# Gate with columns on partitions, bias and gate applied out of PSUM, and rank products ahead of the output products in a recurrence

## What is computed

```python
r = xr @ W_r
log_w = -softplus(-(tanh(xw @ w_lora_a) @ w_lora_b + w_lora_bias)) - 0.5
k = xk @ W_k
v = xv @ W_v
a = sigmoid(xa @ a_lora_a @ a_lora_b + a_lora_bias)
g = sigmoid(r @ g_lora_a) @ g_lora_b + g_lora_bias
...
def step(S, xs):                      # S: (batch, head, 16, 16), 1024 steps
    r_t, w_t, k_t, v_t, a_t, b_t = xs
    sa = einsum('bhij,bhj->bhi', S, a_t)
    S = S * exp(w_t)[:, :, None, :] + sa[..., None] * b_t[:, :, None, :] \
        + v_t[..., None] * k_t[:, :, None, :]
    o_t = einsum('bhij,bhj->bhi', S, r_t)
...
o_flat = ((o - mu) * rsqrt(var + EPS)).reshape(Bn, Tn, C) * gn_weight + gn_bias
bonus = ((rh * kh * r_k).sum(-1, keepdims=True) * vh).reshape(Bn, Tn, C)
return (o_flat + bonus) * g @ W_o
```

## Time and profile before

| | |
|---|---|
| median of 3 runs | 4384.21 us |
| profiled execution | 4389.97 us, its span 4388.2 us |
| PE busy | 3922.4 us (89%) |
| DVE busy | 3172.3 us (72%) |
| ACT busy | 2217.2 us (51%) |
| POOL busy | 2087.8 us (48%) |
| mean granted TensorE clock | 0.938 |
| recurrence: first and last `prod` start | 2234.7 and 3841.4 us |

### The profile page before, as it was taken

How to read it: one execution, slowest core, us unless ns; L and a number is a source line. 1 busy time by engine, 2 the same in 40 slices (tenths; PEclk the granted TensorE clock), 3 DMA queues, 4 the chain that set the end, 5 groups by cost and what they waited for, 6 DMA issues and landing times. The chain is left out here.

```text
span 4388.2 us, 71340 instructions
## 1 busy us (share of the span) xinstructions
PE 3922.4 (89%) x23332; PEld 2675.2 (61%) x23332; DVE 3172.3 (72%) x8603; ACT 2217.2 (51%) x7429; POOL 2087.8 (48%) x1686
## 2 busy tenths in 40 slices
PE   5999999999996599698959999999999999947698
PEld 2344444444344466466648888888888888846465
DVE  5778777777763311599869999999999999957310
ACT  1666666666665311466504655555555556524211
POOL 2212211211212522223358888888888888725322
PEclk7999999999996699799979999999999999977799
DMA  4323322332344332344452232232232322157242
GB/s 111 79 75 78 96 73 66 102 79 59 88 112 135 125 125 85 116 181 174 170 108 36 35 42 36 35 43 35 38 41 35 41 37 35 22 174 250 68 132 79
DMA packets 478766, 378.35 MB, mean 86 GB/s; under 512 B 298348, under 2 KB 440713, under 8 KB 472260
## 3 DMA queue, kind: packets, MB, share of 16 engines
q1 hardware_dynamic: 466116, 348.64, 32.5%
q0 software_dynamic: 12288, 25.28, 1.8%
HBM read 221.87 MB, written 159.58 MB: 87 GB/s over the span
## 5 line engine op out<-in xcount | busy, mean ns | idle before, releaser
L750 DVE TENSOR_REDUCE at_neg_max<-at_slot 128x1 f32<-128x512 f32 (+3 forms) x1216 | 745.8, 655 | 247.9 <-PE at_slot L542 245.1
L672 ACT ACTIVATE at_prob<-at_slot 128x512 f32<-128x512 f32 (+1 forms) x1216 | 631.3, 577 | 356.1 <-PE at_slot L562 355.3
L2157 PE MATMUL sc_added<-sc_outer,sc_ident 128*128 128x128 f32 x4096 | 585.6, 286 | 63.4 <-POOL sc_outer L1908 42.8
L2157 PEld LDWEIGHTS sc_added<-sc_outer,sc_ident 128*128 128x128 f32 x4096 | 496.4, 191 | 193.9 <-DVE sc_state L2058 115.4
L1921 POOL TENSOR_TENSOR sc_terms<-sc_seen,sc_pack 128x1024 f32<-128x1024 f32 (+2 forms) x288 | 603.1, 2137 | 13.7 <-PE sc_ps_o L2179 13.7
L2179 PE MATMUL sc_ps_o<-sc_terms,sc_ident 128*128 128x256 f32 x2048 | 607.0, 381 | 2.1 <-POOL sc_terms L1921 2.1
L390 POOL TENSOR_SCALAR_AFFINE_SELECT at_prob<-at_prob 128x512 f32<-128x512 f32 x256 | 163.5, 639 | 889.3 <-ACT at_prob L672 889.2
L2081 ACT ACTIVATE sc_seen<-sc_state 128x512 f32<-128x512 f32 x256 | 152.9, 597 | 744.0 <-DVE sc_decayed L2022 733.5
L542 PE MATMUL at_slot<-at_k_stack,at_q_stack 96*128 96x512 bf16 (+3 forms) x1536 | 459.5, 335 | 22.5 <-DMA at_k_stack<-parts 20.1
L1908 POOL TENSOR_TENSOR sc_outer<-sc_pack 128x2048 f32<-128x2048 f32 x128 | 467.3, 3672 | 5.0
L562 PE MATMUL at_slot<-at_q_stack,at_k_stack 99*128 99x512 bf16 (+3 forms) x1536 | 452.9, 331 | 12.2 <-ACT at_prob L672 11.8
(11 more groups left out here) (311 smaller groups left out, 7144.5 us busy)
## 6 DMA issues: line engine op xcount, KB each, us to landing
packed<-pr_pack SPq DMA_DIRECT2D x16, 3072.0 KB
sc_pack<-packed SPq DMA_DIRECT2D x512, 96.0 KB, 3.6
parts<-at_parts SPq DMA_DIRECT2D x96, 256.0 KB
f_up_w<-in_ffn_wi SPq DMA_DIRECT2D x16, 1024.0 KB
f_down_w<-in_ffn_wo SPq DMA_DIRECT2D x16, 1024.0 KB
at_q_stack<-parts SPq DMA_DIRECT2D x32, 384.0 KB
at_k_stack<-parts SPq DMA_DIRECT2D x32, 384.0 KB
slots<-at_no_row SPq DMA_DIRECT2D x2, 4128.0 KB
```

Of the source, the lines that this page charges most:

```text
L672: act.activation(prob[:, first:first + n, q1 - tiles * P:q1], ps[:, 0:n * tiles * P].rearrange("p (n k) -> p n k", n=n), ACT.Exp)\
L750: dve.tensor_reduce(neg_max[:, chunk, qt, h:h + n], ps[:, 0:n * tiles * P].rearrange("p (n k) -> p n k", n=n), AX.X, ALU.max, negate=True) ...
L2157: pe.matmul(added[h][:, 0:HALF], ident[:], outer[m % 2][:, 2 * n + s, h * HALF:(h + 1) * HALF], start=(s == 0), stop=False)
```

## The change

In `prepare` the gate is made with columns on partitions: TensorE multiplies the weights `inner_b["g"]` as the stationary operand with all 1024 tokens, one half of the columns per job; ScalarE empties it with the bias as a per-partition column, and it is stored as (batch, half, column, token).

In `finish_and_route` GpSimd has no bias job. VectorE makes o * weight + bonus, TensorE turns it, and VectorE takes each turned piece of 128x512 out of PSUM with (+ bias, * gate) in one operation into `y_turned`; ScalarE copies no longer. The job list is in another order: `y_turn` and `r_turn` before `weigh_o` of the next batch, `place` before `y_out`, `choose` before `affine`.

In `recurrence` (1) on TensorE `rank` comes before both `terms` products of a pair; (2) GpSimd adds the outer products of the two steps for pairs 1 and 3 of each half span, after each half's outer products, and TensorE has one matmul per half state instead of two for these four of eight pairs; (3) ScalarE writes `seen` with i and j exchanged, and GpSimd's product reads and writes in that order, with r repeated along the innermost dimension, where before the output was written with a step of 16.

```diff
 FINISH_SLOTS = 6
-FINISH_USER = {"y_turn": "act", "y_out": "dve", "r_turn": "act"}
+FINISH_USER = {"y_turn": "dve", "y_out": "dve", "r_turn": "act"}
 def finish_plan():
...
         return [(stage, (b, c, half)) for half in range(2) for c in range(KC)]
-    plan = of("bias", 0) + of("weigh_o", 0)
+    plan = of("weigh_o", 0)
     for b in range(BATCH + 2):
-        plan += of("bias", b + 1) + of("weigh_o", b + 1) + of("weigh", b - 2) + parts("y_turn", b) + parts("r_turn", b - 1)
-        plan += of("count", b - 2) + parts("y_out", b) + of("gate", b - 1) + of("place", b - 2) + of("stats", b)
-        plan += of("affine", b) + of("choose", b - 1)
+        plan += of("weigh", b - 2) + parts("y_turn", b) + of("count", b - 2) + parts("r_turn", b - 1) + of("weigh_o", b + 1)
+        plan += of("place", b - 2) + parts("y_out", b) + of("gate", b - 1) + of("stats", b)
+        plan += of("choose", b - 1) + of("affine", b)
     return plan
                 k = b % 2
-                for dst, src in ((o, feed.o_in), (bonus, feed.bonus_in), (og, feed.gate_in)):
+                for dst, src in ((o, feed.o_in), (bonus, feed.bonus_in)):
                     sp.dma_start(dst[k][:], rows(src, b)).then_inc(in_ready[k], 16)
+                sp.dma_start(og[k][:], feed.gate_in[b].rearrange("k p t -> p k t")).then_inc(in_ready[k], 16)
             def load_x(b):
                 sp.dma_start(x[b % XBUFS][:], rows(x_in, b)).then_inc(x_loaded[b % XBUFS], 16)
-            bias_wide = wide_b[:].unsqueeze(1).broadcast_to([P, TILES, C])
-
             for stage, what, s, use in plan.jobs:
-                if stage == "bias":
-                    b = what
-                    if b == 0:
-                        pool.wait_ge(norm_in, 1 + 32)
-                    pool.wait_ge(in_ready[b % 2], 1 + 48 * (b // 2 + 1))
-                    pool.tensor_tensor(bonus[b % 2][:], bonus[b % 2][:], bias_wide, ALU.add).then_inc(with_bias, 1)
-                elif stage == "place":
+                if stage == "place":
                     b = what
...
                     if (c, half) == (0, 0):
-                        pe.wait_ge(gated, 1 + b + 1)
+                        pe.wait_ge(weighed_o, 1 + b + 1)
                     for n in range(HALF_TILES):
...
                     act.activation(exps[b % 2][:], work[:], ACT.Exp).then_inc(exp_ready, 1)
-                elif stage in ("y_turn", "r_turn"):
+                elif stage == "r_turn":
                     b, c, half = what
...
                     if b and (c, half) == (0, 0):
-                        if stage == "y_turn":
-                            slots.wait_read(act, *[("y_out", (b - 1, q)) for q in range(4)])
-                        else:
-                            act.wait_ge(gate_ready, 1 + b)
-                    dst = y_turned if stage == "y_turn" else turned
-                    act.activation(dst[:, c, half * BANK:(half + 1) * BANK], slot[s][:], ACT.Copy)\
+                        act.wait_ge(gate_ready, 1 + b)
+                    act.activation(turned[:, c, half * BANK:(half + 1) * BANK], slot[s][:], ACT.Copy)\
                        .then_inc(emptied[s], 1)
...
                 own.link(dve.tensor_tensor(o[k][:], o[k][:], weight_wide, ALU.mult))
-                dve.wait_ge(with_bias, 1 + b + 1)
-                own.link(dve.tensor_tensor(o[k][:], o[k][:], bonus[k][:], ALU.add))
-                dve.tensor_tensor(o[k][:], o[k][:], og[k][:], ALU.mult).then_inc(gated, 1)
+                dve.tensor_tensor(o[k][:], o[k][:], bonus[k][:], ALU.add).then_inc(weighed_o, 1)
+
+            def gate_y(b, c, half, s, use):
+                slots.wait_filled(dve, s, use)
+                if b and (c, half) == (0, 0):
+                    slots.wait_read(dve, *[("y_out", (b - 1, q)) for q in range(4)])
+                columns = slice(half * BANK, (half + 1) * BANK)
+                dve.scalar_tensor_tensor(out=y_turned[:, c, columns], in0=slot[s][:], scalar=norm_b[:, c:c + 1],
+                                         in1=og[b % 2][:, c, columns], op0=ALU.add, op1=ALU.mult)\
+                   .then_inc(emptied[s], 1)
             def add_x(b, quarter, s, use):
...
         OPS = 10
-        AHEAD = 10
+        AHEAD = 12
+        SUMMED = (1, 3)
         BEHIND = 5
...
                         pack[m % 4][:, t, FK * D:(FK + 1) * D].unsqueeze(2).broadcast_to(shape), ALU.mult))
+                    own.done()
+                    by_steps = outer[m % 2][:, t, :].rearrange("p (a q s) f -> p a q s f", q=2, s=2)
+                    of_pairs = by_steps[:, :, SUMMED[0]]
+                    own.up(pool.tensor_tensor(of_pairs[:, :, 0, :], of_pairs[:, :, 0, :], of_pairs[:, :, 1, :], ALU.add))
                 assert own.n + 2 == AHEAD
...
                     return pool.tensor_tensor(
-                        terms[m % 2][:].rearrange("p (n s) (j i) -> p n s i j", s=2, j=D)[:, pair:pair + n, step],
-                        seen[:, slot:slot + n, :].rearrange("p n (i j) -> p n i j", j=D),
-                        vectors(m, step, FR)[:, pair:pair + n, :].unsqueeze(2).broadcast_to(shape), ALU.mult)
+                        terms[m % 2][:].rearrange("p (n s) (j i) -> p n s j i", s=2, j=D)[:, pair:pair + n, step],
+                        seen[:, slot:slot + n, :].rearrange("p n (j i) -> p n j i", j=D),
+                        vectors(m, step, FR)[:, pair:pair + n, :].unsqueeze(3).broadcast_to(shape), ALU.mult)
                 first = m % 2 * PAIRS
...
                     if pair == 0:
-                        dve.wait_ge(pre, 1 + g * AHEAD + AHEAD - 2)
+                        dve.wait_ge(pre, 1 + g * AHEAD + AHEAD - 4)
                     for h in range(2):
...
                 slot, to = (m * PAIRS + pair) % RING, m % 2 * PAIRS + pair
-                act.activation(seen[:, to:to + 2, :], state[:, slot:slot + 2, :], ACT.Copy).then_inc(copied, 1)
+                act.activation(seen[:, to:to + 2, :].rearrange("p n (j i) -> p n i j", j=D),
+                               state[:, slot:slot + 2, :].rearrange("p n (i j) -> p n i j", j=D), ACT.Copy)\
+                   .then_inc(copied, 1)
             def copy_o(g):
...
                 if n in (0, PAIRS // 2):
-                    pe.wait_ge(pre, 1 + g * AHEAD + AHEAD - 1 + n // (PAIRS // 2))
+                    pe.wait_ge(pre, 1 + g * AHEAD + AHEAD - 2 + n // (PAIRS // 2) * 2)
                 for h in range(2):
                     pe.wait_ge(chain, CHAIN + 1 + (g * PAIRS + n - 1) * OPS + OPS - 1 + h)
-                    for s in range(2):
+                    for s in range(1 if n % (PAIRS // 2) in SUMMED else 2):
                         pe.matmul(added[h][:, 0:HALF], ident[:],
...
                     add_decayed(at[0], n)
+                    add_rank(at[0], n)
                     if behind:
                         add_terms(*behind, 2 * n)
-                    add_rank(at[0], n)
-                    if behind:
                         add_terms(*behind, 2 * n + 1)
...
 PREPARE_USER = {"turn_x": "act", "turn_w": "act", "fold": "act", "r": "act", "w_inner": "act", "g_inner": "act", "w": "act",
-                "a_inner": "act", "g": "dve", "a": "act", "v": "act", "k": "act"}
+                "a_inner": "act", "g": "act", "a": "act", "v": "act", "k": "act"}
 def prepare_start():
...
                     slots.wait_read(sp, ("g", h), alone=True)
-                    sp.dma_start(gate_out[rows].rearrange("n p c -> p n c"),
-                                 gate_sb[h][:].rearrange("p (n c) -> p n c", c=C)).then_inc(gate_stored[h], 16)
+                    sp.dma_start(gate_out[b, h], gate_sb[h][:]).then_inc(gate_stored[h], 16)
                     slots.wait_read(sp, ("v", h), alone=True)
...
                                                  start=(k == 0), stop=(k == KC - 1))
+                    elif stage == "g":
+                        if what == 0:
+                            slots.wait_read(pe, ("g_inner", 0))
+                        for half in range(2):
+                            tokens = slice(half * BANK, (half + 1) * BANK)
+                            last = pe.matmul(ps[:, tokens], inner_b["g"][:, what * P:(what + 1) * P],
+                                             inner["g"][:, tokens], start=True, stop=True)
                     else:
...
                         act.activation(field(what, FV), by_head(ps[:]), ACT.Copy).then_inc(emptied[s], 1)
+                    elif stage == "g":
+                        act.wait_ge(gate_stored[what], 1 + b * 16)
+                        act.activation(gate_sb[what][:], ps[:], ACT.Identity, bias=g_bias_columns[:, what:what + 1])\
+                           .then_inc(emptied[s], 1)
                     elif stage == "k":
...
                         mix(slots, what)
-                    elif stage == "g":
-                        slots.wait_filled(dve, s, use)
-                        dve.wait_ge(gate_stored[what], 1 + b * 16)
```

(2 more changed lines are left out.)

22 lines of the change are left out of this document (13 added, 9 removed).

## The result

The changed kernel took 4335.65 us (median of 4 runs, 4329.1 to 4336.2) against 4384.87 for the kernel before (4 runs) on the same chip: ratio 0.9885, 95% interval 0.9868 to 0.9902, 49 us less. I had forecast 4289, 95 us less; the time lies 10.7 us above the upper end of the range. On another chip (number 11) the same kernel took 4291.3 us against 4363.6: ratio 0.9834, interval 0.9820 to 0.9847, 72 us less. So two things have to be explained: why the gain is smaller than forecast everywhere, and why it differs between the two places.

The account below looks back on a forecast made before the run. Bound: in the recurrence, VectorE's `rank`-to-`state` chain, waiting for TensorE's late rank product. Recurrence -71 + 0.4, finish -21, prepare -3 make -95; 4390 - 95 - 6 = 4289 us, range 4257 to 4325.

Parts of the forecast that it names:

- Recurrence, -71: Rank products first on TensorE: 1.15 us saved against the mean span of 25.1, over 62 full spans.
- from matmul start to `state` it took 0.49, so `state` comes at 2.72: Ordinary recurrence pair: rank matmul starts at about 3002.23, `state` at 3002.72, put at 3002.74 for VectorE's semaphore wait; 0.09 saved.
- The six pairs with the gap: Recurrence pairs with a 0.14 us gap before `state`: 0.09 saved in five, 0.12 with the reciprocal, 0.02 with `from_u`.
- The first pair: First pair of a recurrence span: the 0.61 us wait shrinks to about 0.05; 0.75 us saved there.
- The sums keep the wait from coming back: GpSimd's sums halve the outers behind `from_u` and `from_v`, 0.49 instead of 0.97 us, so TensorE does not overrun.
- What GpSimd pays: GpSimd per recurrence span: sums add 2.8 us, the product at 1.93 saves 1.8; busy 22.6, below VectorE's 23.95.
- mildly the bound: Rival, chance 0.15: GpSimd's product stays at 2.38 us, span 24.4, saving 0.7 per span; kernel 4317 us.
- Finish: Finish stage: VectorE's 5.50 us wait for GpSimd goes; 22.7 us per batch instead of 25.3, -21 over eight batches.
- the new waiting for `y_out`: Finish stage: VectorE, done at 10.7 us, waits 2.7 per batch for TensorE's `r_turn` halves and `y_out`.
- the finish stage gains nothing: Rival, chance 0.12: TensorE at 1.2 GHz takes over 13 us for `y_out`, 25 us per batch stays; kernel 4310.
- Prepare: Prepare stage: gate's addition moves to ScalarE, but `squares` comes 1.0 us later; -0.15 per batch, -2 in the last, -3 together.
- The copy with a step of 16: ScalarE's copy to `seen` in the recurrence: even twice 0.60 us costs zero, at most a tenth of a microsecond per span.

## Why the prediction was right and wrong, point by point

- **Direction**: right; faster, by more than the 0.2% that can be told. The size was wrong by half on the first chip and by a quarter on chip 11.
- **Recurrence, -71 against -32 (and -33.5)**: the step that failed is "from matmul start to `state` it took 0.49, so `state` comes at 2.72". I took a duration measured on a matmul whose weights had been loaded beside other work, and used it for one that starts from idle. It takes 0.60 there. The 0.13 that the array was "held" was in truth the weight load, which the product needs in any case (0.10 longer without cover); 0.02 remained of the 0.09. The six pairs with the gap gave 0.12 a span where I had 0.59, and that sum counts nine pairs: beside the first one and those with `sum_dots`, the reciprocal and `from_u` there are four ordinary ones, not five. So 0.47 a span is missing here, 29 us over 62 spans. The Trainium skill (TensorE: Matmul & The Clock Gate, LDWEIGHTS) gives a load of 128 columns as 128 / 1.2, 107 ns; the trace agrees, with 0.10 between the two lengths (0.71 and 0.61).
- The first pair was taken right in its mechanism (the wait of 0.61 is gone), and too large in size: 0.47 instead of 0.75, 17 us over 62 spans. Of the 46 us missing in both, 11 had been taken off beforehand, when 25.28 was set down to 25.1. The first span became 1.7 us longer (forecast 1.4). The rest of its wait is that same product started from idle (0.56 from the start of the last `rank` to `state` in pair 0, where I had 0.46).
- **The sums keep the wait from coming back**: right in mechanism and place (pair 1), but the overrun is 0.08 and not some tenths, presumably because it can run into the 0.27 that TensorE has free ahead of `rank`; worth 3 us.
- **What GpSimd pays**: right in each number (1.94, 1.27, 1.75 of waiting). The rival "mildly the bound", which rests on 2.38 for the product, is refuted for the product: 1.94 in 171 cases of one stretch. The same goes for the 2.6 cycles per element that the Trainium skill (GPSIMD Engine Reference, Elementwise side-by-side cycle accounting) gives as a floor for two inputs: the trace doesn't agree, as 1.94 us for 1024 elements are 2.3 cycles of 1.2 GHz over the whole operation. The rival's time, though, would have been too low: with the old product the span is 25.07 and not 24.4, by a mechanism that neither I nor the rival had. I had looked at VectorE's large operations for meetings with GpSimd and passed over a 128x16 one.
- **Finish**: -21 forecast, -14.7 and -36.0 measured. On chip 11 the new waiting for `y_out` is 0.55 per batch and not 2.7. Two terms were too large: `y_out`, 8.8, which I took from a stretch at a granted clock of 0.81, took 7.09 at 1.00:

```profile
4003.70:4012.50 8.80, 8.80 (x41) 7.53 (x37) 4.65 (x3) 2.53 (x4) 4.15 (x2) 0.81 1.06 327
...
3903.13:3910.22 7.09, 7.09 (x36) 6.26 (x35) 6.41 (x12) 2.86 (x5) 1.05 (x2) 1.00 1.03 309
```

  (busy time by stretch, before on the first chip, after on chip 11; the last three columns are granted clock, DMA share, GB/s). And the two halves of `r_turn`, 3.88 in the sum, took 3.4 until `y_out` began (3920.16 to 3923.55 on chip 11). Together that is 2.2 less, and the wait fell from 2.7 to 0.55. The start of the stage gave 9 us more (first `tok` 74.9 us after the last `prod` instead of 84.0), which I hadn't counted. On the first chip the late signal took 1.75 to 4.74 us of six batches back: there the 25 us of my rival "the finish stage gains nothing" came true by luck, and not its mechanism: `y_out` took 7.22 at a granted clock of 0.98 and not over 13, and the new wait is another than the one I had named.
- **Prepare**: -3 forecast, -3.5 and -5.0 measured, with the rows as described.
- **The copy with a step of 16**: I had bounded it by twice the time and zero cost; it took 1.76 times, at no cost.
- **Range**: it rested on the bounds of GpSimd, which were the wrong place to be uncertain about; TensorE's 0.49 had no bounds at all.

## What to carry to other kernels

A wait for a busy engine may hide a cost that comes back when the wait goes: before billing the gap ahead of a matmul, look whether its weights are loaded in that gap. Before a chain of clever reliefs is built around an order of instructions, try the order alone: here one moved line gave 31 of the recurrence's 33.5 us. Where GpSimd gets more work, look for the smallest VectorE operation with two SBUF operands that its instructions can meet, and put it where GpSimd waits; and compare stages on more than one chip before a wait without a plausible releaser is explained.

## What the runs showed of the hardware that I had not expected

- Two float32 matmuls of 128x128 (four passes) that start after 0.27 us without a weight load take 0.71, and the first of them signals 0.50 after its start; with the first weights loaded beside another product it is 0.61 and 0.40. Counted from the load's start the signal comes at 0.50 and 0.52.
- A VectorE operation of 16 elements with two SBUF operands takes up to 0.90 us instead of 0.165 when GpSimd is in the middle of a product of 2.4 us: it ends 0.03 us after it.
- In the first measurement, signals from TensorE to VectorE came 3 to 6 us late in most, not all, of the batches in which GpSimd issued indirect DMAs at that time. By comparison with chip 11 that goes with 21 and 18 us more ahead of prepare (kernel before and after), and with some 20 in the finish stage of the new one alone. In the runs on chips 2, 6, 11, 13 and 14 it didn't occur. The cause is open.
- A ScalarE copy of 512 elements from PSUM that writes to SBUF with a step of 16 elements takes 1.05 us instead of 0.60.
